# Attention results turned by VectorE in 32x32 blocks, and loads issued by need, in a one-core transformer layer

## The reference, cut to what matters

```python
def attn(x):                     # x: 2 x 1024 x 128, already layer-normalised
    q, k, v = x @ Wq.T, x @ Wk.T, x @ Wv.T          # split in 16 heads of 8
    q, k = rope(layernorm_per_head(q)), rope(layernorm_per_head(k))
    s = softmax(causal(q @ k.T / sqrt(8)))
    return (s @ v) @ Wo.T + bo
x = x + attn(layernorm(x))
h = layernorm(x)
combine = two_largest_of_gated_groups(softmax(h @ gate_w.T), gate_b)
y = sum_e combine[e] * ((silu(h @ We1[e] + be1) * (h @ We3[e] + be3)) @ We2[e] + be2)
x = x + y + silu(h @ ws1 + bs1) * (h @ ws3 + bs3) @ ws2 + bs2
```

## Time and profile before

| | us |
|---|---|
| median of 3 runs | 390.1 |
| the runs | 388.71, 390.1, 1749.16 |
| the profiled execution | 388.73 |
| its span, first to last instruction | 386.7 |
| PE busy, share of the span | 340.4, 88% |
| DVE busy | 282.6, 73% |
| ACT busy | 240.7, 62% |
| POOL busy | 180.2, 47% |
| mean granted clock of TensorE | 0.95 |

### The profile page before, as it was taken

How to read it: one execution, slowest core, us unless ns; L and a number is a source line. 1 busy time by engine, 2 the same in 40 slices (tenths; PEclk the granted TensorE clock), 3 DMA queues, 4 the chain that set the end, 5 groups by cost and what they waited for, 6 DMA issues and landing times.

```text
span 386.7 us, 8032 instructions
## 1 busy us (share of the span) xinstructions
PE 340.4 (88%) x2931; PEld 150.9 (39%) x2931; DVE 282.6 (73%) x496; ACT 240.7 (62%) x352; POOL 180.2 (47%) x304
## 2 busy tenths in 40 slices
PE   2634388889999999999999999999999999999895
PEld 1322144444554444434443433334343433444332
DVE  5464278948998998788998988788579972168833
ACT  1536314787777768774668785676877899644310
POOL 1165886789894556386631140470301126665000
PEclk9958556999999999999999999999999999999999
DMA  2994700320320005800100512000100006200000
GB/s 78 201 179 89 164 1 14 100 56 3 90 81 3 3 6 150 185 22 0 31 1 2 135 37 54 2 3 2 30 0 30 2 3 159 63 3 0 4 23 27
DMA packets 25687, 19.64 MB, mean 51 GB/s; under 512 B 9585, under 2 KB 22418, under 8 KB 25586
## 3 DMA queue, kind: packets, MB, share of 16 engines
q1 hardware_dynamic: 24258, 18.09, 20.7%
q10 hardware_dynamic: 1392, 1.05, 1.2%
HBM read 11.56 MB, written 1.15 MB: 33 GB/s over the span
## 4 chain that ended last, share of the span: by engine, by line
PE 65%; DVE 12%; DMA 6%; POOL 5%; SPq 4%; issue 3%; ACT 3%; DVEq 0%; ACTq 0%; POOLq 0%
PE psum L705 14%; PE psum L753 12%; PE psum L682 9%; PE psum L769 8%; PE psum L659 8%; PE psum L633 6%; DVE mx_diag L1162 4%; DMA xs<-in_x 3%; PE psum L615 3%; DMA q_st<-parts 1%; SPq L505 1%; DVE mx_full L1162 1%; PE psum L773 1%; ACT probs L835 1%; PE psum L624 1%
## 5 line engine op out<-in xcount | busy, mean ns | idle before, releaser
L835 ACT ACTIVATE probs<-psum 128x1024 f32<-128x1024 f32 x144 | 142.6, 1023 | 42.5 <-PE psum L682 21.5
L1162 DVE TENSOR_REDUCE mx_diag<-psum 128x4 f32<-128x512 f32 (+2 forms) x96 | 96.6, 1043 | 25.9 <-PE psum L659 24.7
L1162 DVE TENSOR_REDUCE mx_full<-psum 128x2 f32<-128x1024 f32 x64 | 76.8, 1222 | 17.7 <-PE psum L659 17.3
L705 PE MATMUL psum<-probs,v_ones 128*18 128x512 f32 (+3 forms) x768 | 75.3, 490 | 0.0
L753 PE MATMUL psum<-x2T,w 128*128 128x512 f32 x144 | 71.4, 612 | 1.1 <-ACT mv L898 1.1
L633 PE MATMUL psum<-masks 64*128 64x128 bf16 (+2 forms) x896 | 51.2, 215 | 12.7 <-DMA q_st<-parts 5.6
L659 PE MATMUL psum<-k_st,q_st 62*128 62x512 bf16 (+3 forms) x384 | 59.5, 341 | 1.2 <-DVE mv L1241 0.8
L682 PE MATMUL psum<-q_st,k_st 64*128 64x512 bf16 (+3 forms) x384 | 53.4, 327 | 2.3 <-DVE mx_diag L1162 0.9
L633 PEld LDWEIGHTS psum<-masks 64*128 64x128 bf16 x896 | 33.6, 96 | 44.8 <-DVE mx_diag L1162 14.3
L1080 POOL TENSOR_SCALAR mh<-mh 128x512 f32<-128x512 f32 x27 | 16.7, 620 | 45.5 <-ACT mh L888 45.5
L1087 POOL TENSOR_TENSOR mh<-mh,mv 128x512 f32<-128x512 f32 x27 | 34.2, 1269 | 7.5 <-DVE mv L1241 7.0
(11 more groups left out here) (166 smaller groups left out, 366.7 us busy)
## 6 DMA issues: line engine op xcount, KB each, us to landing
early<-combine_scratch SPq DMA_DIRECT2D x24, 256.0 KB, 4.9
q_st<-parts SPq DMA_DIRECT2D x24, 128.0 KB, 3.0
k_st<-parts SPq DMA_DIRECT2D x18, 128.0 KB, 2.4
w<-in_We SPq DMA_DIRECT2D x3, 512.0 KB
k_st<-in_c_pad SPq DMA_DIRECT2D x2, 512.0 KB, 11.1
out<-xs SPq DMA_DIRECT2D x4, 256.0 KB, 2.3
xs<-in_x SPq DMA_DIRECT2D x3, 256.0 KB, 13.0
k_st<-parts ACTq DMA_DIRECT2D x6, 128.0 KB, 4.0
```

The source lines that it names most:

```text
L705: last = pe.matmul(acc[32 * j:32 * j + 2 * VC, q0:q0 + cols], own_then_zeros, probs[:, n % P_RING, j % 2, col:col + cols], start=(kt == 0 ...
L835: act.activation(probs[:, n % P_RING, :, :], wpair("scores", (s, i)), ACT.Exp, scale=SCALE).then_inc(exp_done, 1)
L1162: dve.tensor_reduce(dst[:, a % 2, :, pairs[0]:pairs[0] + nm, qt], w, AX.X, ALU.max, negate=True).then_inc(max_free, 1)
```

## The change

Attention results: ACT's copy, both PE turns and ACT's second copy go. `oturn.n` (DVE) turns the accumulator's 32x32 blocks each in its own place, PSUM to o_turned; reciprocal and product then work from o_turned to o_norm, and `oback.x` (DVE) turns the 32x32 blocks of o_norm to o_normT. A block of the accumulator holds one group of rows for 32 queries, so turning each block where it stands, once out and once back, leaves o_normT with one row per channel.

```diff
+            def take_blocks(n):
+                dve.wait_ge(pv_done, max(q for q, (a, _) in enumerate(BURSTS) if a == 2 * n + 1) + 1)
+                if n:
+                    dve.wait_ge(o_normed, n)
+                dve.transpose(o_turned[:, :], bank(ACC_BANK)).then_inc(o_taken, 1)
             def normalise(n):
-                dve.wait_ge(work_full, turned("oT", n))
+                dve.wait_ge(o_taken, n + 1)
                 if pair == 0 and x:
-                    dve.wait_ge(work_full, turned("onT", x - 1))
-                w = wbank("oT", n).rearrange("p (n v) -> p n v", v=32)[:, :, 0:2 * VC]...
+                    dve.wait_ge(o_back, x)
+                w = o_turned[:, :].rearrange("p (n v) -> p n v", v=32)[:, :, 0:2 * VC]...
+            def turn_back(x):
+                dve.wait_ge(o_normed, NG // 2 * (x + 1))
+                if x:
+                    dve.wait_ge(work_full, turned("proj", x - 1))
+                dve.transpose(o_normT[:, :], o_norm[:, :]).then_inc(o_back, 1)
# pv(s), first burst of a pair from the second pair on
-                    pe.wait_ge(o_ready, a // 2)
+                    pe.wait_ge(o_taken, a // 2)
# project(x)
-                pe.wait_ge(work_read_act, frees("act", FILL["onT", x] + 1))
+                pe.wait_ge(o_back, x + 1)
# on ACT
-            def leave(n):
...
-                act.copy(o_raw[:, :], bank(ACC_BANK)).then_inc(o_ready, 1)
```

```diff
-        N_ATTN, N_ROPE, N_PAD, N_MOE = 7, 6, 4, 15
+        N_ATTN, N_ROPE, N_PAD, N_REST, N_MOE = 5, 5, 4, 11, 15
-            for w, dst in ((Wq, 0), (Wk, 1), (Wv, 2), (Wo, 3)):
+            for w, dst in ((Wq, 0), (Wk, 1), (Wv, 2)):
...
-            sp.dma_start(bo_b[:, :], bo.partition_broadcast(P)).then_inc(ld_rope, 16)
+            sp.dma_start(xs[:, 1, :, :], x_v[B]).then_inc(ld_x[1], 16)
             sp.dma_start(masks...).then_inc(ld_causal, 16)
+            for t in range(N_TERMS, HD):
+                pad(k_st[t::HD, 0, :, 0:CH], ld_pad)
+                pad(q_st[t::HD, 0, :, :], ld_pad)
+            for i in range(2, NX):
                 sp.dma_start(xs[:, i, :, :], ...).then_inc(ld_x[i], 16)
+            for t in range(N_TERMS, HD):
+                pad(k_st[t::HD, 0, :, CH:S], ld_rest)
+                for c in range(2):
+                    pad(k_st[t::HD, 1, :, c * CH:(c + 1) * CH], ld_rest)
+                pad(q_st[t::HD, 1, :, :], ld_rest)
+            sp.dma_start(w_raw[:, 3, :], Wo).then_inc(ld_rest, 16)
+            sp.dma_start(gate_raw[:, :], gate_w).then_inc(ld_rest, 16)
+            sp.dma_start(bo_b[:, :], bo.partition_broadcast(P)).then_inc(ld_rest, 16)
             sp.dma_start(rank[:, :], c_rank).then_inc(ld_moe, 16)
# weights2 (PE), the maxima of unit 4 (PE) and xbo.0 (POOL)
+                pe.wait_ge(ld_rest, 16 * N_REST)
```

More of the change, by code:

```diff
@@ L132 @@
 ORDER = """
[L133 to L142, removed]
@@ new lines @@
+maxred.5.2 max.5.3@45 maxred.5.3 pv.4 pv.5 oturn.0 scores.7.1@23 max.5.4@45 maxred.5.4 scores.8.0@01 exp.7.1 xbo.0
+qT.2@6 mrow.3 exp.8.0 scores.9.0@23 oT_read.0 max.5.5@45 maxred.5.5 qT_lead.2 qT_rest.2 scores.9.1@01 pv.6 exp.9.0
+exp.9.1 max.6.0@45 max.6.1@23 maxred.6.0 scores.10.0@01 kT.2@6 exp.10.0 maxred.6.1 mrow.4 scores.10.1@45 max.6.2@23
+maxred.6.2 max.6.3@01 kT_lead.2 exp.10.1 pv.7 rstd_pool.3 max.6.4@45 scores.11.0@23 exp.11.0 maxred.6.3 maxred.6.4
+max.6.5@01 stack.2.1.0 maxred.6.5 stack.2.0.0 pv.8 mneg.5 pv.9 max.7.0@45 qT_mid.2 kT_rest.2 kT_mid.2 stack.2.1.1
@@ new lines @@
+max.7.1@23 scores.12.0@01 exp.12.0 pv.10 pv.11 maxred.7.0 maxred.7.1 mturn.5@4 mcopy.5 oturn.1 oT_read.1 oback.0
+scores.12.1@01 exp.12.1 scores.13.0@45 exp.13.0 max.7.2@23 maxred.7.2 rope_pool.3 scores.13.1@01 proj.0@6 proj_read.0
+norm2.0 exp.13.1 scores.14.0@23 exp.14.0 mrow.5 scores.15.0@01 max.7.3@45 pv.12 scores.15.1@23 exp.15.0 exp.15.1
+maxred.7.3 stack.2.0.1 max.7.4@01 qT_low.2 kT_low.2 mneg.6 mturn.6@6 max.7.5@45 scores.16.0@23 maxred.7.4 exp.16.0
+stack.2.0.2 stack.2.1.2 max.8.0@01 mcopy.6 maxred.7.5 maxred.8.0 norm2_rstd.0 norm2_apply.0 max.8.1@23 max.8.2@45 mneg.7
@@ new lines @@
+stack.3.1.1 exp.31.0 moeU.1.2@2 moe_t.1.2 stack.3.0.0 route2.1 moe_a.1.2 moeV.1.3@3 moe_v.1.3 scores.31.1@45 exp.31.1
+max.10.7@01 maxred.10.7 moe_y.0.4 moe_h.0.8 moe_y.0.5 moeU.1.3@2 moeU.1.4@4 moe_one.1.2 moe_g.1.1 moe_g.1.2 moe_t.1.3
+moeU.1.5@5 route3.1 moe_one.1.3 moe_t.1.4 moe_t.1.5 moeV.1.4@3 moe_v.1.4 moeV.1.5@1 moe_v.1.5 moe_y.0.6 moe_a.1.3
+scores.32.0@23 exp.32.0 moe_a.1.4 max.10.8@01 qT_low.3 moe_a.1.5 moe_y.0.7 max.10.9@23 max.10.10@45 maxred.10.8
+maxred.10.9 maxred.10.10 moe_y.0.8 y_leave.0 scores.32.1@01 exp.32.1 max.10.11@23 maxred.10.11 pv.29 max.10.12@45
@@ L255 @@
+moe_y.3.3 moeL.3.8@4 moe_s.3.8 moe_m.3.8 moe_y.3.4 moe_y.3.5 moe_h_dve.3.8 moe_y.3.6 moe_y.3.7 moe_y.3.8 y_leave.3
+yturn.3@2 final.3 store.3
 """
@@ L343, in layer_kernel @@
         probs = sb("probs", [P, P_RING, 2, CH])
-        o_raw = sb("o_raw", [P, CH])
+        o_turned = sb("o_turned", [P, CH])
         rden = sb("rden", [P, 2, TPC * G, 2, 1])
-        o_norm = sb("o_norm", [P, TPC, P])
+        o_norm = sb("o_norm", [P, CH])
         o_normT = sb("o_normT", [P, CH])
@@ L645, in maxima @@
                     pe.wait_ge(ld_pad, 16 * N_PAD)
+                if a == NG and u == 0:
+                    pe.wait_ge(ld_rest, 16 * N_REST)
                 if u == 0:
@@ L797, in _ @@
                     pv(arg)
-                elif kind == "oT":
-                    pe.wait_ge(o_ready, arg + 1)
-                    turn(kind, arg, lambda t: o_raw[:, t * P:(t + 1) * P])
-                elif kind == "onT":
-                    pe.wait_ge(work_read_dve, frees("dve", turned("oT", NG // 2 * arg + NG // 2 - 1)))
-                    turn(kind, arg, lambda t: o_norm[:, t, :])
                 elif kind == "proj":
```

243 lines of the change are left out of this document (109 added, 134 removed).

## The result

The changed kernel takes **383.4 us** (median of 4 runs, 383.2 to 384.4) against 389.4 us for the kernel before beside it: ratio 0.985, 95% interval 0.984 to 0.987. The ratio leaves out the kernel before's one run of 1749.16 us, which lies far from its other three (388.4 to 390.1), while the median of 389.4 counts it. The kernel is faster by some 5.6 us, clear of noise, where I had forecast 14. By the prediction's own bar of 2% that is no change, to which it had given 0.26. The profiled execution has a span of 381.7 us against 386.7.

What follows compares the result with a forecast made beforehand. PE's own work was taken to bound the kernel from 80 us on, after an idle start and a stretch shared with DVE. 388.7 - 7.6 + 2.0 - 6.1 - 3.1 + 0.6 + 1.1 = 375.6, predicted 376 us, range 367 to 388.

Steps and rivals of the forecast that it cites:

- the prediction's own bar of 2%: Whole kernel: a time within 2% of 390.1 us, 382.3 to 397.9, counts as no change; chance 0.26.
- the prediction's own signs of being wrong: First maximum later than 46 us, PE idle from 80 us on up over 4 us, or transposes over 1 us.
- The start: Up to the attention's opening: loads reordered by need open it at 42.0 us instead of 48.1, -6.1 us.
- -3.1: Before attention: two projections of chunk 2, 1.58 and 1.57 us at half clock, leave the chain, -3.1 us.
- The turns: PE after 80 us: 32 transposes of o_raw (5.1 us) and 16 of o_norm (2.5 us) go, -7.6 us.
- VectorE, +2.0: DVE: twelve new transposes at 0.69 us, 8.3 us in all, a quarter of it on the time, +2.0 us.
- Reciprocal and product stay: DVE: beside the new transposes these two operations stay; no time was added for them.
- DVE becomes the bound: Rival, middle of the kernel: all 8.3 us of transposes land, 381.9 us, or 388.3 at 1.22 us each; 15%.
- The late start: Rival, start: SP's loads end 4 to 5 us later, attention opens at 47 us, total 383.7 us; 18%.
- The tail: Between last projection and x2T: PE's filler is 5.1 us against a chain of 6.2 us, +1.1 us.
- The hand-over: Rival, accumulator bank: a transpose queued behind DVE's reductions frees it, so the next pv waits; up to 401.5 us; 8%.
- The clock: Rival, 48.1 to 64 us: PE may run at clock 1.00 instead of 0.50, 6 us more gain, 370 us; 11%.

Runs made afterwards that it cites:

- x of chunks 2 and 3 late: The changed kernel with the loads of x of chunks 2 and 3 moved behind the eight pads the opening does not need: 386.5 us, ratio 0.992.
- the two experiments: The changed kernel with each of its 12 VectorE transposes issued twice, 391.1 us; and with each cut to 32 columns, 381.2 us.
- the route alone: The kernel before with only the new route of the attention results (VectorE transposes), in the old order and with the old loads: 398.7 us, ratio 1.025.
- chunk 1 late: The changed kernel with x of chunk 1 issued behind the opening's pads, ahead of x of chunk 2: 384.5 us, ratio 0.990.

## Why the prediction was right or wrong

The sign was right and the time lies in the range. The forecast itself (371 to 381) missed: the sum was off by 8 us against the profiled execution's 383.6, in three terms, and less than half of the gain came. One of the prediction's own signs of being wrong came true: PE's idle time from 80 us on grew by more than 4 us, by 4.6 up to 320 us alone.

- **The start: right in sum, by two errors that cancel.** Forecast -6.1, -3.1 and +0.6 for the turn of Wo and the gate's weights, together -8.6; measured -8.9. The chain from the loads to the turn of q and k held as forecast, and x of chunks 2 and 3 late undid 4.5 us of it. The opening came 1.9 us sooner than forecast, since SP's loads ended at 29.86 and the 1.4 us for their issue were not due; the stacks, which did not run alone, took some of it back. Against that, -3.1 was too much: it priced the two projections at the half clock (1.58 and 1.57 us). The half clock lasted as long as before, and other work stood in it, so only their full-clock price, half of that by estimate, was gained. The other 1.6 us, due behind the opening, did not come, and stand against those 1.9.
- **The turns, -7.6: mis-sized, -5.9.** The earlier trace rows give busy time, 281 ns a matmul with overlapping ends. In the stages' starts a turn of four costs 0.49 us of PE, not 0.63: twelve are 5.9. The time at which the next stage starts is what counts.
- **VectorE, +2.0: the first failed step.** Behind the opening the table has +5.3. The duration was right:

```profile
L1165 DVE STREAM_TRANSPOSE o_turned<-psum 128x512 f32<-128x512 f32 x8 | 5.7, 714 | 9.8 <-PE psum L718 9.7
L1176 DVE TENSOR_TENSOR o_norm<-o_turned,rden 128x256 f32<-128x256 f32 x8 | 5.5, 690 | 0.3
L1182 DVE STREAM_TRANSPOSE o_normT<-o_norm 128x512 f32<-128x512 f32 x4 | 2.8, 709 | 0.1
```

  0.71 us each against 0.69 taken; twelve are 8.5. The share was wrong: a quarter, argued from DVE's idle time, where the two experiments show about one for one up to 251 us. DVE's idle time was there, but not where the transposes stand, between reductions that PE's next maximum waits for. "Reciprocal and product stay" was wrong too: the product now reads SBUF, and its 424 ns became 690 on average (up to 1157), 2.1 us more in all; where GpSimd's two-input work ran beside it in the route alone, one took 1.40. In the kernel before, four of the eight ran beside such work with one operand in PSUM, and all took 424 or 425 ns. My rival "DVE becomes the bound" had this mechanism; with all 8.3 us charged it gave 381.9. The late start gave 383.7, nearer still, but what it describes did not happen: that number is luck.
- **The tail, +1.1: the second failed step,** +4.7. I looked for filler that PE has between proj.3 and x2T.3 and took the chain on DVE at its 6.1 us. The chain itself became longer, 7.9 us, by 1.8 of exclusion with GpSimd, and the wait was 3.3 us. The new order made most of that good elsewhere: at full clock, with chunk 1 late, the tail would be +1.5. The larger part is the clock, which I had put at nothing: 3.2 us. In the kernel before neither showed, because GpSimd happened to be idle from 340.8 to 344.1.
- **The hand-over, 8%:** PE's waits in the changed kernel name o_turned nowhere, as forecast; but the route in the old order has 3.5 us in two of them and was slower than before. It was a real danger that the new order avoids.
- **The clock, 11%: wrong.** Behind the opening it stayed at 0.50 until 56.84 us, 16.8 us long, as before (16.3 us, 48.1 to 64.4).
- The rule on the transposes (the Trainium skill, page "VectorE: DVE Perf Modes", section "The three transpose paths") gave an estimate of 1.24 us for 512 columns by scaling; measured 0.71. A figure for one tile is not to be multiplied by four: 32 columns took 0.21, so 480 more took 0.50.
